# Two rows per block in the first and the last normalisation, with block-diagonal pair and router weights

## The reference

```python
# layer 1: attention in each row, with a bias that all rows share
n = layernorm(_ln_c(x)) * gamma + beta             # over the 64 channels
q, k, v = n @ Wq * C ** -0.5, n @ Wk, n @ Wv       # 4 heads of 32
pair_bias = n @ Wb                                 # 64 -> 4, one number per head
attention = softmax(k q + mask_bias + pair_bias)
x = x + (attention @ v * sigmoid(n @ Wu + bu)) @ Wo * mask
# layer 2: a recurrence; layer 3: a state-space scan in both directions
# layer 4: mixture of experts
n = _ln_t(x)
p = softmax(n @ router_w + router_b)               # 64 -> 8 experts, best 2 taken
x = x + sum over the best 2 of p_e * (n @ expert_w[e] + expert_b[e])
```

## Time and profile before

| | us |
|---|---|
| median of three runs | 2875.82 (2871.61 to 2888.48) |
| the profiled execution | 2882.99 |
| its span in the profile | 2881.2 |
| first normalisation, first turn to last pair product | 16.8 to 76.5 |
| attention's rows | 81 to 582 |
| second normalisation (recurrence) | 583 to 619 |
| third normalisation (state space) | 759 to 796 |
| last normalisation, first turn to last router product | 2626.6 to 2689.3 |
| choice of experts, then the experts | 2690 to 2717, 2717 to 2881 |

### The profile page before, as it was taken

The page is one execution under the profiler, slowest core; times in us unless marked ns, Lnnn a source line. Parts: engine busy times, 40 slices in busy tenths (PEclk is TensorE's granted clock), DMA queues, the critical chain, the costliest instruction groups (busy, mean ns, idle before and its releaser), DMA issues. The chain is left out here.

```text
span 2881.2 us, 39692 instructions
## 1 busy us (share of the span) xinstructions
PE 2554.3 (89%) x9720; PEld 1331.6 (46%) x9720; DVE 2243.6 (78%) x2423; ACT 1903.6 (66%) x3872; POOL 1942.7 (67%) x1102
## 2 busy tenths in 40 slices
PE   7899999957559999999999869999999999998598
PEld 7566666724324343443443324444444444446422
DVE  4465665660639999999999939899899899995599
ACT  7566665643658788787787748777777777775221
POOL 3232332330339999999999948898898899894255
PEclk9899999969679999999999989999999999998799
DMA  3000000000246666766676636666666666660022
GB/s 62 10 9 7 9 9 9 6 1 0 46 131 228 222 230 226 225 227 227 218 225 231 223 118 217 207 220 223 205 213 222 207 213 220 219 207 20 17 55 46
DMA packets 168089, 404.30 MB, mean 140 GB/s; under 512 B 64614, under 2 KB 69195, under 8 KB 168012
## 3 DMA queue, kind: packets, MB, share of 16 engines
q1 hardware_dynamic: 149580, 395.02, 43.3%
q10 hardware_dynamic: 18432, 8.39, 1.2%
HBM read 370.84 MB, written 24.12 MB: 137 GB/s over the span
## 5 line engine op out<-in xcount | busy, mean ns | idle before, releaser
L1499 POOL TENSOR_TENSOR sb_hc<-sb_h,sb_cc 128x1024 f32<-128x1024 f32 x256 | 602.4, 2368 | 90.5 <-PE sb_py L1259 79.0
L1499 POOL TENSOR_TENSOR sf_hc<-sf_h,sf_cc 128x1024 f32<-128x1024 f32 x256 | 601.3, 2364 | 53.0 <-PE sf_py L1259 33.0
L1259 PE MATMUL sf_py<-sf_hc,ident 128*128 128x512 f32 x1024 | 496.5, 611 | 0.0
L1259 PE MATMUL sb_py<-sb_hc,ident 128*128 128x512 f32 x1024 | 493.4, 608 | 0.5 <-DVE sb_yo L1544 0.5
L1580 DVE TENSOR_TENSOR_SCAN sf_h<-sf_dA,sf_state,sf_pu 128x1024 f32<-128x1024 f32 x192 | 446.3, 2339 | 19.0 <-PE sf_pu L1237 7.8
L1580 DVE TENSOR_TENSOR_SCAN sb_h<-sb_dA,sb_state,sb_pu 128x1024 f32<-128x1024 f32 x192 | 444.7, 2336 | 9.3 <-ACT sb_dA L1409 1.2
L575 POOL TENSOR_TENSOR ar_sc<-ar_sc,ar_mx 128x512 f32<-128x512 f32 x128 | 154.8, 1209 | 351.6 <-DVE ar_mx L516 351.6
L1259 PEld LDWEIGHTS sf_py<-sf_hc,ident 128*128 128x128 f32 x1024 | 179.4, 191 | 203.5 <-issue 201.3
L1259 PEld LDWEIGHTS sb_py<-sb_hc,ident 128*128 128x128 f32 x1024 | 178.3, 190 | 201.8 <-issue 194.2
L1409 ACT ACTIVATE sf_dA<-sf_dt,ss_A 128x1024 f32<-128x1024 f32 x192 | 219.1, 1143 | 1.4 <-issue 1.2
L1409 ACT ACTIVATE sb_dA<-sb_dt,ss_A 128x1024 f32<-128x1024 f32 x192 | 219.1, 1143 | 0.9
(11 more groups left out here) (312 smaller groups left out, 5116.2 us busy)
## 6 DMA issues: line engine op xcount, KB each, us to landing
sf_cc<-rows_scratch SPq DMA_DIRECT2D x256, 512.0 KB, 4.5
sb_cc<-rows_scratch SPq DMA_DIRECT2D x256, 512.0 KB, 4.2
sf_bb<-rows_scratch SPq DMA_DIRECT2D x64, 512.0 KB, 5.4
sb_bb<-rows_scratch SPq DMA_DIRECT2D x64, 512.0 KB, 5.1
sf_n<-n_scratch SPq DMA_DIRECT2D x32, 258.0 KB, 5.4
sb_n<-n_scratch SPq DMA_DIRECT2D x32, 258.0 KB, 5.3
y_scratch<-sf_yo SPq DMA_DIRECT2D x16, 512.0 KB, 5.4
sb_yf<-y_scratch SPq DMA_DIRECT2D x16, 512.0 KB, 6.2
```

The costliest lines, as they stand in the source:

```text
L1259: ins = nc.tensor.matmul(p_y[:, hf], lhsT=c.ident[:, :], rhs=hc[:, s % RING, hf], start=(s == 0), stop=(s == U - 1))
L1499: nc.gpsimd.tensor_tensor(hc[:, s % RING, :], h[:, s % RING, :], cc[:, s % C_RING, :], ALU.mult).then_inc(read, 1)
```

## The change

In `norm_stage`, callers with `use` now get two neighbouring rows in one 128-column piece. `out` holds 4 pieces per block instead of 8, GpSimd writes the same 512 numbers side by side, TensorE turns 4 pieces per block and ScalarE evacuates one group of 128 x 512 per block. `xT` becomes 128 partitions x 8,192: rows 0, 2, 4, ... on the lower 64 partitions, 1, 3, 5, ... on the upper. The second evacuation into `xg` is gone; `pair` and `route` read `xT`. Their weights are twice as wide and block-diagonal (`Wb` twice in a 128 x 8 tile, the router's in 128 x 16), so that one product gives both rows. TensorE's loop over the blocks is written out. Where `use` isn't given nothing moves, but the zeros behind `out` are no longer written. The router's bias is no longer a row of ones: two matmuls of 512 columns write it to all of `er_ps` first, and the products add to it. Gamma, beta and the weights are loaded to both halves of the partitions. The later copies to `xg` become two transfers per group, one for the even and one for the odd rows, in pieces of 128 tokens (512 bytes).

```diff
+def rows_of_half(eng, dst, xT, g, landed):
+    for a in range(2):
+        eng.dma_start(dst.rearrange("d (p a q) -> d p a q", a=2, q=Q)[:, :, a, :],
+                      xT[a * D:(a + 1) * D, bass.ds(g * (GT // 2), GT // 2)].rearrange("d (p q) -> d p q", q=Q)
+                      ).then_inc(landed, 16)
...
-    GPC = R // GR
+    GPC = 1 if use is not None else R // GR
...
-        out = sb("_out", [Q, RING, R, 2, D])
+        out = sb("_out", [Q, RING, R if use is None else R // 2, 2, D])
...
-            with eng.Fori(2, NCH // RING) as i:
-                body(i, lambda j: lambda lag: True)
+            if unrolled:
+                for i in range(2, NCH // RING):
+                    body(i, lambda j: lambda lag: True)
+            else:
+                with eng.Fori(2, NCH // RING) as i:
+                    body(i, lambda j: lambda lag: True)
...
-            if wide == 1:
-                nc.gpsimd.memset(out[:, :, :, 1, :], 0.0).then_inc(set_, 1)
...
-        xT = sb("at_xT", [D, T])
+        xT = sb("at_xT", [128, T // 2])
...
+                for a in range(2):
+                    half = slice(a * D, (a + 1) * D)
+                    sp.dma_start(gamma[half, :], col_of(A["gamma"])).then_inc(affine_loaded, 16)
+                    sp.dma_start(beta[half, :], col_of(A["beta"])).then_inc(affine_loaded, 16)
+                    sp.dma_start(wb[half, a * HEADS:(a + 1) * HEADS], A["Wb"]).then_inc(affine_loaded, 16)
+                sp.wait_ge(affine_loaded, 96)
...
-                nc.scalar.activation(xg[0:D, slot, :], ps[0:D, :], ACT.Identity, bias=beta[:, :], scale=gamma[:, :])
-                return nc.scalar.activation(xT[:, bass.ds(g * GT, GT)], ps[0:D, :], ACT.Identity,
-                                            bias=beta[:, :], scale=gamma[:, :])
+                return nc.scalar.activation(xT[:, bass.ds(g * GT, GT)], ps, ACT.Identity, bias=beta[:, :],
+                                            scale=gamma[:, :])
...
-                    nc.tensor.matmul(pairs[:, bass.ds(g * GR + j, 1), :].rearrange("p a e -> p (a e)"),
-                                     lhsT=xg[:, slot, j * Q:(j + 1) * Q], rhs=wb[:, :],
+                    nc.tensor.matmul(pairs[:, bass.ds((g * GR + j) * 2, 2), :].rearrange("p a e -> p (a e)"),
+                                     lhsT=xT[:, bass.ds((g * GR + j) * Q, Q)], rhs=wb[:, :],
                                      start=True, stop=True).then_inc(paired, 1)
...
-                sp.dma_start(xg[0:D, k, :], xT[:, bass.ds(g * GT, GT)]).then_inc(g_loaded[k], 16)
+                rows_of_half(sp, xg[0:D, k, :], xT, g, g_loaded[k])
...
         def router_there():
-            nc.tensor.wait_ge(ones_set, 1)
-            nc.tensor.wait_ge(weights_loaded, 32)
+            nc.tensor.wait_ge(ones_set, 3)
+            nc.tensor.wait_ge(weights_loaded, 48)
+            for a in range(2):
+                nc.tensor.matmul(routes[:, a * (S // 2):(a + 1) * (S // 2), :].rearrange("p a e -> p (a e)"),
+                                 lhsT=ones[:, :], rhs=br[:, :, :].rearrange("b a e -> b (a e)"), start=True,
+                                 stop=True, skip_group_check=True)
```

More of the change, by code:

```diff
@@ L125, in norm_stage, with run @@
         shaped = lambda t: t.rearrange("q (a r) d -> q a r d", a=halves)
-        def run(eng, step):
+        def run(eng, step, unrolled=False):
             def body(i, has):
@@ L217, in step @@
                     src = cen[:, b, :, :, :].rearrange("q a r d -> q r a d")
-                    nc.gpsimd.tensor_tensor(out[:, b, :, 0:wide, :], src.to_broadcast(shape) if twice else src, rstd,
+                    dst = (out[:, b, :, 0:wide, :] if use is None else
+                           out[:, b, :, :, :].rearrange("q p a d -> q (p a) d").rearrange("q r (z d) -> q r z d", z=1))
+                    nc.gpsimd.tensor_tensor(dst, src.to_broadcast(shape) if twice else src, rstd,
                                             ALU.mult).then_inc(scaled, 1)
             nc.gpsimd.memset(add[:, :], var_add).then_inc(set_, 1)
-            if wide == 1:
-                nc.gpsimd.memset(out[:, :, :, 1, :], 0.0).then_inc(set_, 1)
             run(pool, step)
@@ L248, in step @@
                         pe.wait_ge(taken, g + 1)
-                        use(g, (j * GPC + b) % RING)
-            if wide == 1:
-                pe.wait_ge(set_, 2)
+                        use(g)
             if before is not None:
                 before()
-            run(pe, step)
+            run(pe, step, use is not None)
 def attention_stage(nc, c, A, x_in):
@@ L269, in attention_stage @@
         ones = sb("at_ones", [1, 128])
-        gamma, beta = sb("at_gamma", [D, 1]), sb("at_beta", [D, 1])
+        gamma, beta = sb("at_gamma", [128, 1]), sb("at_beta", [128, 1])
         mask, maskT = sb("at_mask", [128, 128]), sb("at_maskT", [128, 128])
@@ L295, in _ @@
             def _(sp):
-                sp.dma_start(gamma[:, :], col_of(A["gamma"])).then_inc(affine_loaded, 16)
-                sp.dma_start(beta[:, :], col_of(A["beta"])).then_inc(affine_loaded, 16)
-                sp.dma_start(wb[0:D, :], A["Wb"]).then_inc(affine_loaded, 16)
-                sp.wait_ge(affine_loaded, 48)
+                for a in range(2):
[4 more added lines that the diff above has]
+                sp.wait_ge(affine_loaded, 96)
             @block.gpsimd
             def _(pool):
-                nc.gpsimd.memset(wb[D:128, :], 0.0).then_inc(padded, 1)
+                nc.gpsimd.memset(wb[0:D, HEADS:2 * HEADS], 0.0).then_inc(padded, 1)
+                nc.gpsimd.memset(wb[D:128, 0:HEADS], 0.0).then_inc(padded, 1)
                 nc.gpsimd.memset(xg[D:128, :, :], 0.0).then_inc(padded, 1)
-                pool.wait_ge(padded, 2)
+                pool.wait_ge(padded, 3)
                 nc.gpsimd.memset(xg[D:D + 1, :, :], 1.0).then_inc(padded, 1)
-                pool.wait_ge(padded, 3)
+                pool.wait_ge(padded, 4)
         with ExitStack() as bctx:
@@ L437, in project @@
             def project(g, k, which, pair):
-                pe.wait_ge(g_loaded[k], 16 * (pair + 1))
+                pe.wait_ge(g_loaded[k], 32 * (pair + 1))
                 need(pe, g_taken, 2 * g + which)
@@ L1709, in experts_stage, with evacuate, route @@
         ones_set = c.sem("ex_ones")
-        def evacuate(g, ps, slot):
-            need(nc.scalar, routed, GR * (g - SLOTS + 1))
-            nc.scalar.copy(xg[0:D, slot, :], ps[0:D, :])
-            return nc.scalar.copy(xT[0:D, bass.ds(g * GT, GT)], ps[0:D, :])
-        def route(g, slot):
+        def evacuate(g, ps):
+            return nc.scalar.copy(xT[:, bass.ds(g * GT, GT)], ps)
+        def route(g):
             for j in range(GR):
-                nc.tensor.matmul(routes[:, bass.ds(g * GR + j, 1), :].rearrange("p a e -> p (a e)"),
-                                 lhsT=xg[0:D + 1, slot, j * Q:(j + 1) * Q], rhs=wr[:, :],
-                                 start=True, stop=True).then_inc(routed, 1)
+                nc.tensor.matmul(routes[:, bass.ds((g * GR + j) * 2, 2), :].rearrange("p a e -> p (a e)"),
+                                 lhsT=xT[:, bass.ds((g * GR + j) * Q, Q)], rhs=wr[:, :],
+                                 start=False, stop=True, skip_group_check=True).then_inc(routed, 1)
         def router_there():
-            nc.tensor.wait_ge(ones_set, 1)
-            nc.tensor.wait_ge(weights_loaded, 32)
+            nc.tensor.wait_ge(ones_set, 3)
[4 more added lines that the diff above has]
+                                 stop=True, skip_group_check=True)
         with ExitStack() as wctx:
@@ L1732, in _ @@
             def _(sp):
-                sp.dma_start(wr[0:D, :], W["router_w"]).then_inc(weights_loaded, 16)
-                sp.dma_start(wr[D:D + 1, :], row_of(W["router_b"])).then_inc(weights_loaded, 16)
+                for a in range(2):
+                    sp.dma_start(wr[a * D:(a + 1) * D, a * EXPERTS:(a + 1) * EXPERTS],
+                                 W["router_w"]).then_inc(weights_loaded, 16)
+                sp.dma_start(br[:, :, :], W["router_b"].rearrange("(a b e) -> a b e", a=1, b=1).to_broadcast(
+                    [1, S // 2, EXPERTS])).then_inc(weights_loaded, 16)
             @block.gpsimd
             def _(pool):
-                nc.gpsimd.memset(xg[D:D + 1, :, :], 1.0).then_inc(ones_set, 1)
+                nc.gpsimd.memset(wr[0:D, EXPERTS:2 * EXPERTS], 0.0).then_inc(ones_set, 1)
+                nc.gpsimd.memset(wr[D:128, 0:EXPERTS], 0.0).then_inc(ones_set, 1)
+                nc.gpsimd.memset(ones[:, :], 1.0).then_inc(ones_set, 1)
         norm_stage(nc, c, "ex_n", 1.0, 1e-5, evacuate, more_loads=load_weights, more_sets=set_ones, before=router_there,
@@ L1833, in group @@
                 def group(g, k, i):
-                    pe.wait_ge(loaded[k], 16 * (i + 1))
+                    pe.wait_ge(loaded[k], 32 * (i + 1))
                     for j in range(GR):
```

22 lines of the change are left out of this document (11 added, 11 removed).

## The result

| | before | changed |
|---|---|---|
| time, us, median (lowest to highest) | 2875.18 (2871.61 to 2888.48, 4 runs) | 2833.92 (2827.30 to 2843.28, 4 runs) |
| ratio, 95% interval | | 0.985 (0.981 to 0.989) |
| profiled execution (span) | 2882.99 (2881.2) | 2843.28 (2841.5) |

A forecast was written before the change was run, and what follows sets the result against it. TensorE and ScalarE were taken as joint bounds, VectorE next. Gains of 27.2 (first stage) and 31.7 (last normalisation) less 0.55 for loads gave 58.3, so 2818 us against the median 2875.82; range 2810 to 2848.

The forecast's parts named there:

- What bounds the kernel: First and last normalisation: TensorE and ScalarE at the limit together, 10.00 and 9.83 of 10 us; a block takes 3.57.
- the work halved: Both stages: TensorE's block falls from 3.57 to 1.79 us; ScalarE, with one evacuation instead of four, needs about 1.5.
- VectorE next: Both stages: VectorE becomes the bound at 1.9 us a block, as in the second normalisation, 27.52 for 16 blocks.
- The stage's length: Both stages: 27.5 us from first turn to last scaling, plus 3.5 tail (last turns 0.93, three blocks' products 2.6).
- Bias matmuls: Before the last normalisation's turns: two router bias matmuls, 4.1 us for both, ending a good 1 us before the first turn.
- The start: Program start: three more load issues before the input's load delay it by 1.4 us, bounds 1.2 to 1.9.
- The loads: Split 512-byte loads: 0 in attention, with landing assumed 2.8 us after issue; +0.55 us at the experts' start.
- Rival D: Attention: split loads land later than 6.0 us after issue, TensorE waits in all 32 groups; 2890 us, chance 0.03.
- The clock: Both stages: the whole sum supposes TensorE at 2.4 GHz; at 1.2 GHz a block would need 3.4 us.
- Forecast A: Both changed stages run with TensorE at 2.4 GHz: 2818 us, chance 0.60.
- rival B: One of the two stages stays at or falls to 1.2 GHz: +23 us, less if midway; 2841, chance 0.28.
- the row at 75 us: Old first stage's end: in a run of products alone the clock fell from 0.89 to 0.50 though TensorE never stopped.

The follow-up runs named there:

- The best version: Changed kernel with 128-column products, VectorE's loop written out, products a block earlier, and small loads on ScalarE's queue beside the input's load: 2820.4 us, ratio 0.978.
- its own experiment: Kernel before, with only each group's load for attention and the experts split into two in 512-byte pieces: 2878.6 us, ratio 1.000.
- the run without the gap: Changed kernel with VectorE's loop in the first and last normalisation written out, products still 8 or 16 columns: 2826.3 us, ratio 0.980.
- wide products: Changed kernel with each pair and router product moving 128 columns, zero-padded, instead of 8 or 16: 2823.1 us, ratio 0.980; also used with a longer gap, 2830.9.
- all five thin runs with a gap: Products of 8 or 16 columns: changed kernel (2833.92, again 2838.3); with VectorE's loop written out, two extra VectorE sums (2843.4, again 2849.4) or four (2857.3).

## Why the prediction was right or wrong

**What bounds the kernel; the work halved; VectorE next.** Right. Where the clock is 1.00, VectorE is at 10.00 of 10 in both stages and a block takes 1.9. The second normalisation was the right model of the rate.

**The stage's length, 27.5 + 3.5 = 31.0 from the first turn.** Low by 1.4: 32.4 in the last normalisation and 32.8 in the first stage with VectorE's loop written out (17.94 to 50.76). The 27.5 up to GpSimd's last scaling was right (2617.19 to 2644.70 in the last normalisation), and so was 2.6 for the products of three blocks. The mis-sized term is the last block's turns: they ended 2.3 after the last scaling (at 2646.99) where 0.93 was taken, since TensorE was still at the turns of the block before (from 2644.06) and by its order had a block's products to make in between. In the first stage the last 24 passes took 3.34 on top of that, since the clock fell within them.

**Bias matmuls.** Right: 3.75 for a bound of 4.1, hidden with 1.85 to spare.

**The start.** +1.6 for a term of 1.4 within bounds of 1.2 to 1.9. One pair of executions doesn't fix it that closely: the first sum came at 10.5 to 11.0 in the eight profiled executions with the changed start, and at 9.4 and 9.2 in the two with the old. The best version shows that the whole of it, and 3 us more of the old start, was to be had.

**The loads.** Right: in attention each half lands 2.0 after its issue, the second is issued 0.6 behind the first, so both are there after 2.6 for an assumed 2.8, and no wait; at the experts the first matmul comes 0.5 later after its load's issue (2.8, 2677.41 to 2680.23, for 2.3), for a term of 0.55, and router and experts together still took 191.6. Rival D is out by its own experiment. What no run had shown now has a row: 64 KB in 512-byte pieces land in 2.0 where 128 KB in 2 KB pieces took 2.2 (the experts' whole loads). By the Trainium skill (DMA: Bandwidth & Descriptors, "Why small descriptors are slow (HBM only)") transfers from SBUF to SBUF don't suffer the penalty of small descriptors; these rows agree.

**The clock.** This is the step that failed. Forecast A said both stages at 2.4 GHz, 0.60; what happened is rival B, 0.28, in its "less if it falls midway" form: the first stage fell at about 35 us and ended at 65.35 instead of 49.3, 16.1 late. Against the run without the gap (47.05 from the first turn to the last product, and 32.82) the gap and the fall cost 14.2 of them, not 23; the other 1.8 are the stage's length above. Of the 58.3 that the sum promised the profiled execution shows 39.7; 16.1 of the missing 18.6 are the first stage, the rest attention's 2.9 and the last normalisation's 1.3, less small gains elsewhere. That 2834 lies within the range is because the range reached over B, which had 0.28; and that it lies 7 below B's 2841 is luck, since the clock fell midway and not at the start. B's price, turns and thin products mixed at half speed at 3.4 a block, was right to the digit: 8 turning and 8 product passes took 3.4 (58.37 less 54.96, the starts of two groups of turns). What would set the fall off, B had not named. Two things in the reasoning were off. I took the changed stages to be without gaps because the second normalisation is, and passed over VectorE's slow subtraction at 37.01 in the trace of before: hidden there, it had to show once VectorE set the pace. And I gave the rule on idle gaps of the Trainium skill (TensorE: Matmul & The Clock Gate, "Why this matters for your kernels") for A, though the row at 75 us already said that thin products lose the clock with no gap. The runs show that both count: in the first stage gaps of 0.59 and 0.97 cost nothing with wide products, and 0.52 was enough once with thin ones. The rule named the gap; whether the products around it were thin or wide decided as much.

What stays open: why the first stage was lost in all five thin runs with a gap, while the last normalisation kept the clock at 0.68 and 0.96 and lost it only at 2.00. Its products have 16 columns, not 8, while its gap stood as long after the rise (7.7 us for 8.0); no run gives the two stages the same columns, so the columns may be the reason or something else in the stage. Also open is how often the first stage falls without a gap, since only two thin executions without one have a trace of it; both kept the clock until their last run of products.

## What to carry to other kernels

When a change makes another engine the bound, look for every hiccup of that engine in the old trace, hidden or not: each becomes a gap of the engines behind it. Where TensorE mixes turns with very narrow products, judge its clock by counting the passes of a stretch (87 or 48 in 10 us here), and try to keep it by making the products wide with zeros if a pass costs the same anyway: here that was worth 15 us in the changed kernel and 41 in the best version. Work that is halved by doing it in half the passes can lose the gain again at half the clock.

## What the runs showed of the hardware

- **A loop's entry on VectorE** cost about 1.1 us (0.40 of issue, then 1.35 for an operation of 0.69) in the first normalisation of all five kernels that were profiled with the loop, and nothing where it is written out. The same loop in the last normalisation of the changed kernel has no such row (subtractions at 2627.04 and 2629.04, both 0.69). The traces' DMA records have a lead: in all five an instruction fetch of 8,192 bytes (queue q14) starts 0.6 us into the slow subtraction (at 31.21 in the changed kernel, 37.62 before), and from 2626.6 to 2633 there is none. With the loop written out such fetches stand at 31.01 and 34.06 and VectorE does not stall. Whether the fetch is VectorE's, and the cause, isn't shown.
- **Zero columns are almost free**: 8 product passes with 128 moving columns took 1.06 us, with 8 columns 0.96; 24 in a row took 2.84 and, with 16 columns, 2.75.
- **The same kernel differs by attention's clock.** In the changed kernel's execution, and in that with wide products, attention over the same 50 us:

```profile
130.00:180.00 50.00, 48.98 (x237) 34.19 (x236) 26.81 (x84) 28.91 (x75) 14.32 (x12) 0.86 0.03 7
```

```profile
130.00:180.00 50.00, 48.96 (x278) 34.59 (x275) 30.69 (x95) 33.12 (x85) 16.36 (x14) 1.00 0.04 8
```

Attention, the same code in both, took 508.5 and 493.6; over all profiled executions of kernels with the changed attention it was 493.6 to 509.1. Such dips came at another place each time. They go with the spread of one kernel's runs: of 13 runs of the kernel before, the fastest (2870.3) had a mean granted clock of 0.953 and the slowest (2891.3) 0.943. The +2.9 of attention in the first table is within what they make.
